# A graph attention layer on one core: TensorE multiplies the second masks one step later, and mask slots are freed by their readers

## The reference, cut to what matters

```python
# x: 8192 x 128, adj: 8192 x 8192 of 0 and 1, 4 heads of 32
mask  = (adj + eye) > 0
Wh    = (x @ W.T).reshape(n, 4, 32)
sl, sr = einsum('nhd,hd->nh', Wh, a_l), einsum('nhd,hd->nh', Wh, a_r)
e     = sl[:, :, None] + sr.T[None, :, :]          # n x heads x n
e     = where(e >= 0, e, 0.2 * e)
alpha = softmax(where(mask[:, None, :], e, -inf), axis=2)
out   = elu(einsum('nhm,mhd->nhd', alpha, Wh).reshape(n, 128))
y     = layernorm(x + out)
```

## Time and profile before

| | |
|---|---|
| median of three runs | 1832.99 us |
| the profiled execution | 1831.45 us |
| its span, first to last instruction | 1829.7 us |
| DVE busy | 1762.7 us, 96% |
| ACT busy | 1744.1 us, 95% |
| TensorE busy, matmuls | 1655.1 us, 90% |
| mean granted TensorE clock | 0.972 |
| DMA queue of SP | 414.8 MB, 69.2% of 16 engines |

### The profile page before, as it was taken

How to read it: one execution, slowest core, us unless ns; L and a number is a source line. 1 busy time by engine, 2 the same in 40 slices (tenths; PEclk the granted TensorE clock), 3 DMA queues, 4 the chain that set the end, 5 groups by cost and what they waited for, 6 DMA issues and landing times.

```text
span 1829.7 us, 81511 instructions
## 1 busy us (share of the span) xinstructions
PE 1655.1 (90%) x37063; PEld 1620.2 (89%) x37063; DVE 1762.7 (96%) x2090; ACT 1744.1 (95%) x1885; POOL 44.4 (2%) x26
## 2 busy tenths in 40 slices
PE   6088899899999999999998999999998999999995
PEld 6088799899998999999998999999998999989895
DVE  5779999999999999999999999999999999999997
ACT  4699999999999999999999999999999999999993
POOL 1000000000001000010001000010000100010000
PEclk8599999999999999999999999999999999999998
DMA  6979867777776867676777877677777767676221
GB/s 209 360 258 357 282 225 247 234 239 253 230 230 223 268 226 248 227 245 225 234 240 225 267 227 247 214 249 236 245 233 249 238 203 268 219 244 192 60 69 35
DMA packets 240408, 420.05 MB, mean 230 GB/s; under 512 B 14400, under 2 KB 104896, under 8 KB 238016
## 3 DMA queue, kind: packets, MB, share of 16 engines
q1 hardware_dynamic: 240064, 414.83, 69.2%
HBM read 397.48 MB, written 17.30 MB: 227 GB/s over the span
## 4 chain that ended last, share of the span: by engine, by line
issue 79%; ACT 8%; DMA 5%; PE 5%; POOL 2%; DVE 2%; SPq 0%; POOLq 0%; ACTq 0%; DVEq 0%
ACT bmask L400 6%; PE psum L323 3%; DMA abuf<-in_adj_dram 2%; POOL vrs L744 2%; DMA vring<-v_scratch 1%; PE psum L277 1%; DMA v_scratch<-vt 1%; ACT acache L368 1%; PE psum L286 0%; POOL vrs L741 0%; ACT vt L373 0%; DVE acache L504 0%; DVE vt L510 0%; PE trp L310 0%; DVE acache L495 0%
## 5 line engine op out<-in xcount | busy, mean ns | idle before, releaser
L400 ACT ACTIVATE bmask<-lrow,rtab 128x1024 fp8e4<-128x1024 f32 x1480 | 1627.8, 1410 | 9.2 <-PE psum L323 9.1
L323 PE MATMUL psum<-vring,bmask 128*128 128x99 bf16 x16384 | 826.0, 208 | 68.6 <-DVE acc L582 23.3
L323 PE MATMUL psum<-vring,cmask 128*128 128x99 bf16 x16384 | 831.8, 209 | 22.7 <-DVE cmask L576 17.1
L323 PEld LDWEIGHTS psum<-vring,bmask 128*128 128x128 fp8e4 x16384 | 761.3, 97 | 82.4 <-issue 44.8
L323 PEld LDWEIGHTS psum<-vring,cmask 128*128 128x128 fp8e4 x16384 | 762.5, 98 | 38.4 <-DVE cmask L576 29.2
L576 DVE TENSOR_TENSOR cmask<-acache,bmask 128x1024 int32<-128x1024 int32 x512 | 623.9, 1218 | 12.2 <-PE psum L323 11.6
L570 DVE TENSOR_TENSOR bmask<-bmask,acache 128x1024 int32<-128x1024 int32 x512 | 624.4, 1219 | 10.8 <-ACT bmask L400 7.8
L558 DVE TENSOR_SCALAR bmask<-lrow,rtab 128x1024 fp8e4<-128x1024 f32 x568 | 416.1, 748 | 0.0
L368 ACT CAST acache<-trp 128x512 int32<-128x512 f32 x256 | 210.3, 821 | 4.7 <-PE trp L310 4.6
L310 PE MATMUL trp<-pack,abuf 128*128 128x32 bf16 x4096 | 144.0, 177 | 51.3 <-ACT acache L368 36.5
L310 PEld LDWEIGHTS trp<-pack,abuf 128*128 128x128 bf16 x4096 | 126.8, 97 | 55.4 <-issue 20.2
(11 more groups left out here) (59 smaller groups left out, 202.1 us busy)
## 6 DMA issues: line engine op xcount, KB each, us to landing
abuf<-in_adj_dram SPq DMA_DIRECT2D x256, 1024.0 KB, 8.2
vring<-v_scratch SPq DMA_DIRECT2D x512, 198.0 KB, 3.7
lrow<-l_scratch SPq DMA_DIRECT2D x16, 1024.0 KB, 11.1
v_scratch<-vt SPq DMA_DIRECT2D x16, 792.0 KB, 9.8
bmask<-in_x_dram SPq DMA_DIRECT2D x16, 256.0 KB, 3.0
late<-in_x_dram SPq DMA_DIRECT2D x32, 128.0 KB, 4.2
out_dram<-late SPq DMA_DIRECT2D x32, 128.0 KB, 5.1
l_scratch<-cmask SPq DMA_DIRECT2D x1, 128.0 KB, 3.7
```

Of the source, the lines that this page charges most:

```text
L323: return nc.tensor.matmul(psum[:, bank, at * S3:(at + 1) * S3], mask[:, i, j * P:(j + 1) * P], vring[:, q % 4, i, col:col + S3], start=ope ...
L400: last = nc.scalar.activation(bmask[:, q % 4, h, i], lrow[:, p, h], ACT.Relu, bias=rtab[:, t, H + hh:H + hh + 1], scale=BIG, saturate=False)
```

## The change

The products of the second masks leave the step in which the mask is made: at step `q` TensorE multiplies the first masks of `q`, turns pairs, and then multiplies the second masks of `q - 1`. At step 0 of a pass there is no such product, and at step 31 it takes those of 30 and of 31. `mm_done` is still raised behind the second products, and still counts them by step. The comparisons no longer wait for `mm_done` of step `q - 4`; ACT waits for `half_done` and for `c_ready` of it, and DVE for `half_done` (its own XOR of that step is earlier in its list). The waits of `mask_c`, `load_v`, `load_block` and the sums are as before.

```diff
+            def second_products(q):
+                pe.wait_ge(c_ready, q + 1)
+                for i in range(2):
+                    for h in range(HP):
+                        for j in range(SUB):
+                            last = product(q, cmask[:, q % 2, h], (HP + h) * SUB + j, i, h, 1, j)
+                last.then_inc(mm_done, 1)
+
             def step(q):
...
                 last.then_inc(half_done, 1)
                 for r in TURNED[q]:
                     turn_pair(r)
-                pe.wait_ge(c_ready, q + 1)
-                for i in range(2):
-                    for h in range(HP):
-                        for j in range(SUB):
-                            last = product(cmask[:, q % 2, h], (HP + h) * SUB + j, i, h, 1, j)
-                last.then_inc(mm_done, 1)
+                if s > 0:
+                    second_products(q - 1)
+                if s == STEPS - 1:
+                    second_products(q)
...
@@ compare(q) on ACT
-                wait(act, mm_done, q - 3)
+                wait(act, half_done, q - 3)
+                wait(act, c_ready, q - 3)
@@ compare(q) on DVE
-                wait(dve, mm_done, q - 3)
+                wait(dve, half_done, q - 3)
```

More of the change, by code:

```diff
@@ L311, in turn_pair, with product @@
                 last.then_inc(tr_done, 1)
+            def product(q, mask, item, i, h, b, j):
+                c, p, s = WHERE[q]
+                w = c * NP + p
+                bank, at = item // PB, item % PB
+                opening = s == 0 and i == 0 and at == 0
+                if opening:
+                    wait(pe, bank_free, BANKS * (w - 1) + bank + 1)
+                col = (h * 2 + b) * S3
+                return nc.tensor.matmul(psum[:, bank, at * S3:(at + 1) * S3], mask[:, i, j * P:(j + 1) * P],
+                                        vring[:, q % 4, i, col:col + S3], start=opening, stop=True, skip_group_check=True)
+            def second_products(q):
[5 more added lines that the diff above has]
+                last.then_inc(mm_done, 1)
             def step(q):
                 c, p, s = WHERE[q]
[L315 to L324, removed]
                 pe.wait_ge(v_in[q % 4], 16 * (q // 4 + 1))
@@ L330, in step @@
                         for j in range(SUB):
-                            last = product(bmask[:, q % 4, h], h * SUB + j, i, h, 0, j)
+                            last = product(q, bmask[:, q % 4, h], h * SUB + j, i, h, 0, j)
                 last.then_inc(half_done, 1)
```

## The result

The changed kernel takes 1996.85 us, the median of four runs (1991.63 to 2003.98), against 1832.53 us: 1.0906 times the time before, 95% interval 1.0887 to 1.0924. The forecast was 1976 us, in a range of 1865 to 2060. The profiled execution took 1991.63 us, its span is 1989.8 us, 160.1 us more than before. A time here is the median of a kernel's runs; one run of an experiment (e9, 1973.28 us) is left out of its median, since it lies over 1.5% above the fastest run of the same kernel.

A forecast was written before the change was run, and what follows sets the result against it. DVE and ACT were taken to set the pace, with TensorE close behind. Terms of 87 (tables) + 37 (first pass) + 20 (clock) + 1 (end) = 145 us on 1831.45 us gave 1976 us, range 1865 to 2060.

The forecast's parts named there:

- The wait that moves by a step: SP's load_v: tables and blocks go out a step later, TensorE waits for tables; 87 us in 14 passes.
- The wait per table: TensorE, passes 1 to 14: 1.1 us at each of 83 loads at steps 11 to 31, 4.2 us at step 7.
- The spare that takes part of it up: TensorE's spare of 2.4 and 6.8 us a pass absorbs part of 10.8 us of waits, leaving 8.4 and 4.0 us.
- The rival that had none of the spare used: TensorE's spare takes up none of the table waits: 151 us instead of 87, 2040 us in all; chance 0.06.
- The first pass and the clock: First pass: blocks in serial rounds of 12.2 us, 37 us more; lower clock after waits, 1.4 us for each of ten rounds.
- The clock later: Step 7 of the 14 later passes: lower TensorE clock after waits of 3 to 4 us, 0.5 us each.
- a rival at 2092 us: Every TensorE wait drops the clock: 83 x 1.4 = 116 us more, 2092 us; chance 0.05.
- The second slots: DVE's mask_c held 0.7 us by later second products: no cost of its own, otherwise 0 to 1 us a pass.
- the 0.9 us a pass of the rival: Loads come in time and only mask_c's hold remains, 0.9 us in each of 16 passes: 1845 us; chance 0.05.
- The waits that go: ACT's wait of 3.7 us for TensorE at the comparisons should vanish; worth 0 to 3.7 us, taken as 0.

The follow-up runs named there:

- e9: e4 with three cmask slots instead of two: 1948.93 us (1.0633).
- e1: The kernel before, with load_v waiting for mm_done q-2 instead of q-3, so tables and blocks go out one step later: 2006.83 us (1.0984).
- e3: The changed kernel with five tables instead of four and load_v waiting for mm_done q-4: 1863.18 us (1.0168).
- e4: The changed kernel with the block issued ahead of the table in SP's list: 1991.0 us (1.0866).
- e8: The changed kernel with three second slots (cmask), but its four tables: 1997.74 us (1.0923).
- e5: The changed kernel with five tables and three second slots (cmask), mask_c waiting for mm_done q-2: 1831.26 us (1.0).
- e6: The kernel before with only the changed slot waits of the comparisons, TensorE's order as before: 1829.94 us (0.9993).
- e7: The kernel before with the changed slot waits of the comparisons and five tables: 1824.42 us (0.9963).

## Why the prediction was right

- **The wait that moves by a step**: right, shown by e1 (the edit to SP's wait alone gives the loss) and e3 (a fifth table takes 134 us of it away).
- **The wait per table**: the kind of wait is right, the size too large. At steps 11 to 31 TensorE waits 72 us in 71 waits, where 83 of 1.1 us were forecast. At step 7 it waits 22 us in 12 waits, where 14 of 4.2 us were forecast, and the longest of all is 2.9 us: these loads land 8.6 us after issue on average, not 10.2. By the forecast's own formula that is 8.6 - 6.0 = 2.6 us of waiting, but the 14 loads have 1.5 us on average, so TensorE came to them later than its bare steps would. Another 5 us fall at step 20, which the forecast did not have. So the waits are 99 us, not 151.
- **The spare that takes part of it up**: the step of the sum that failed. "Seven passes of each are 87 us" came from 151 us less TensorE's spare of 2.4 and 6.8 us a pass, 64 us in all. In the changed kernel the passes grew by 100.6 us on 98.7 us of waits, and TensorE's other waits did not shrink (61.6 us, 57.5 before). The spare was also taken too large: the earlier trace rows has TensorE busy for 87.07 of 88.22 us and for 88.24 of 92.63 us, which leaves 1.2 and 4.4 us. What did come out as forecast is the difference between the two kinds of pass, 4.7 and 9.7 us (forecast 4.0 and 8.4). But it shows in the waits: 5.9 us a pass where p is 0, 8.2 where p is 1. At step 11 a table wait is 0.1 us on average in the first kind and 1.15 us in the second. The rows don't show why; one reason that fits is that DVE's sums and layer norm make TensorE itself late there. The rival that had none of the spare used was right in this and wrong in size (2040 us), since it took the 151 us.
- **Luck**: waits 52 us too large and a deduction of 64 us that didn't come nearly cancel, 87 us against 100.6. The total came out near by that luck. In e4, where each wait was sized rightly and the deduction was made, the forecast missed by 85 us.
- **The first pass and the clock**: 37 us of serial rounds and 14 us for the clock in them were forecast, 56.7 us came; a round takes 13.1 us in the rows, forecast 12.2 + 1.4. The lower clock follows the waits of about 5 us (0.77 in the stretch, 2.83 us for the block of products behind the wait of 4.66 us, and 2.38 us for the next, where 1.59 is usual).
- **The clock later**: 6 us were taken, and TensorE is busy 6 us longer in the 14 passes. Beside 90 short table waits, the clock record shows the lower level only eight times in them, three times before; the clock is 1.00 and 0.98 in the two passes shown. The Trainium skill's rule in "TensorE: Matmul & The Clock Gate" (Part 1), that the gate falls back to half rate when TensorE is idle, agrees with the waits of 5 us. Read as a price on every wait, which was a rival at 2092 us, it does not hold here.
- **The second slots**: "no cost of its own" is right for the changed kernel (e8), not for e4. The cost by itself was too low, whether it is read as 0 to 1 us or as the 0.9 us a pass of the rival: e3 and e5 give 32 us, 2 us a pass.
- **The waits that go**: 0 taken, and e6 can't tell its 2 us from nothing.

## What to carry to other kernels

Before moving a block of work behind another, list every wait on the semaphore that it raises, above all those that the edit doesn't touch: here the DMA queue's. A load's slack is counted in steps between its release and its use, and the load to look at is the one queued behind the largest transfer, not the median one: all table loads before have a median of 3.7 us from issue to landing, those behind a block 7.7 us. Where two engines are full and the third nearly so, don't deduct the third's idle time from a new wait without a run that shows it; here at most a third of it could be used.

## What the runs showed that was not expected

A table load issued 2.5 to 3.9 us behind a block in the same queue lands about when the block does (0.5 us behind its second transfer in the earlier trace rows). At steps 11 to 31 that is 9.1 to 11.7 us after the block's issue before (mean 10.3), and 8.9 to 11.4 us after the change (mean 10.1); the fastest table load of all lands 2.3 us after its own issue. The lower clock level cost 1.2 us on one block of 32 products after a wait of 4.66 us, and 0.8 us more on the block behind it. And an extra 1584 bytes per partition, the fifth table, together with the new slot waits, was worth 7.5 us to the kernel before (e7).
